# A decoder layer's expert stage: the experts' rows gathered by halves of the blocks, behind chosen stores

## The reference

```python
probs = softmax(xn @ Wr + br)                  # 8 experts
scores, idx = top_k(probs, 2)                  # two experts for each row
full = expert outputs relu(xn @ W1_e + b1_e) @ W2_e + b2_e
c = einsum('ef,efh->eh', relu(b1), W2) + b2;  c_total = c.sum(0)
out = sum(scores * (full[idx] - c[idx] + c_total))
return layernorm(x + residual + out)
```

## Time and profile before

| | us |
|---|---|
| median of 3 runs | 765.85 (764.94 to 766.87) |
| profiled execution | 768.75 |
| its span, first to last instruction | 767.0 |
| TensorE busy | 700.7 (91%) |
| VectorE busy | 472.1 (62%) |
| ScalarE busy | 332.5 (43%) |
| GpSimd busy | 265.8 (35%) |

### The profile page before, as it was taken

One profiled execution on the slowest core, in us unless ns is written; L12 is line 12 of the kernel. 1 busy time (PEld: TensorE's weight loads), 2 busy tenths in 40 slices (PEclk: granted clock), 3 DMA queues, 4 the chain that ended last, 5 costly groups with the idle time before them and its releaser, 6 DMA issues.

```text
span 767.0 us, 15113 instructions
## 1 busy us (share of the span) xinstructions
PE 700.7 (91%) x5090; PEld 610.8 (80%) x5091; DVE 472.1 (62%) x1094; ACT 332.5 (43%) x994; POOL 265.8 (35%) x216
## 2 busy tenths in 40 slices
PE   7799999999999999998998979999999999997980
PEld 7788897888989798896887858888888888786760
DVE  2635446577868778687858745555555555553476
ACT  5575767576676767676430212221222222121112
POOL 1200000120505033050546375176069300438664
PEclk9899999999999999999799899999999999998965
DMA  9367495641011020103141245255134411213125
GB/s 311 100 222 257 146 302 175 202 147 43 30 37 47 16 63 9 43 28 124 57 165 32 73 137 166 68 156 167 34 123 129 145 41 35 68 36 97 56 69 157
DMA packets 68496, 82.66 MB, mean 108 GB/s; under 512 B 5932, under 2 KB 59736, under 8 KB 68440
## 3 DMA queue, kind: packets, MB, share of 16 engines
q1 hardware_dynamic: 59800, 52.54, 21.4%
q0 software_dynamic: 8640, 29.38, 12.1%
HBM read 45.04 MB, written 36.86 MB: 107 GB/s over the span
## 4 chain that ended last, share of the span: by engine, by line
PE 73%; DVE 7%; ACT 7%; POOL 5%; issue 4%; DMA 2%; another core or an unknown queue 1%; POOLq 0%; SPq 0%; DVEq 0%; ACTq 0%
PE bank L1012 14%; PE bank L760 8%; PE bank L761 7%; PE bank L762 7%; PE bank L982 5%; PE bank L984 5%; PE bank L983 5%; PE bank L880 4%; PE bank L992 4%; PE bank L919 3%; PE bank L931 3%; ACT arena L1112 3%; POOL arena L729 2%; PE bank L968 1%
## 5 line engine op out<-in xcount | busy, mean ns | idle before, releaser
L1012 PE MATMUL bank<-w_ring,hidT_hi 128*128 x320 | 121.6, 413 | 6.2 <-DVE hidT_lo L1665 6.2
L1233 ACT ACTIVATE hidT_hi<-bank 128x512 fp32r<-128x512 f32 x80 | 43.5, 596 | 180.6 <-PE bank L992 171.0
L1112 ACT ACTIVATE arena<-bank,negmx 128x128 f32<-128x128 f32 x256 | 90.8, 377 | 6.2 <-DVE negmx L1268 6.2
L1012 PE MATMUL bank<-w_ring,hidT_lo 128*128 x320 | 84.2, 283 | 0.0
L1638 DVE TENSOR_TENSOR arena<-bank,b_rep 128x512 f32<-128x512 f32 x80 | 55.4, 692 | 42.9 <-PE bank L984 41.3
L1644 DVE TENSOR_REDUCE work<-bank 128x256 f32<-128x512 f32 x40 | 27.7, 692 | 85.1 <-PE bank L1012 77.5
L1012 PEld LDWEIGHTS bank<-w_ring,hidT_hi 128*128 128x128 f32 x320 | 61.1, 191 | 18.2 <-issue 6.9
L982 PE MATMUL bank<-w_ring,xgT_hi 128*128 x160 | 67.3, 421 | 4.6 <-DVE xgT_lo L1657 2.8
L632 POOL TENSOR_TENSOR rsq<-ssq,neghalf 128x8 f32<-128x8 f32 x8 | 13.2, 1646 | 145.4 <-DVE ssq L1368 145.4
L984 PE MATMUL bank<-w_ring,xgT_lo 128*128 x160 | 63.5, 397 | 0.0
L983 PE MATMUL bank<-w_ring,xgT_hi 128*128 x160 | 63.2, 395 | 0.0
(11 more groups left out here) (253 smaller groups left out, 1897.3 us busy)
## 6 DMA issues: line engine op xcount, KB each, us to landing
xg_dram<-zeros SPq DMA_DIRECT2D x9, 2176.0 KB, 8.8
w_raw<-in_L_ffn_W_dram POOLq DMA_DIRECT2D x16, 1024.0 KB, 6.1
y_dram<-zeros SPq DMA_DIRECT2D x2, 2560.0 KB, 10.7
work<-xg_dram SPq DMA_DIRECT2D x40, 128.0 KB, 2.1
y_dram<-work SPq DMA_DIRECT2D x40, 128.0 KB, 1.7
b_rep<-in_L_ffn_b_dram POOLq DMA_DIRECT2D x8, 512.0 KB, 4.2
work<-gmax_dram SPq DMA_DIRECT2D x14, 256.0 KB, 3.4
arena<-in_x_dram SPq DMA_DIRECT2D x8, 256.0 KB, 2.7
```

Of the source, the lines that this page charges most:

```text
L1012: last = pe.matmul(o, l, r, start=c == 0 and l is both[0], stop=c == FC - 1 and l is both[0])
L1112: last = nc.scalar.activation(probs[:, n % 2, h * S:(h + 1) * S], ps_score[:, h * S:(h + 1) * S], ACT.Exp, bias=negmx[:, n % 2, h:h + 1], ...
```

## The change

- GpSimd reads its counts before it waits for the weights of the last expert. There are now sixteen: for each half of the blocks (0 to 7, 8 to 15), each k and each of the four store semaphores.
- The low gathers of each half wait for the tile with that half's last row of expert 6, the high gathers for that of expert 7. Nothing waits for all 40 stores but a last wait at the end.
- GpSimd weighs three blocks of four (12 instead of 10). VectorE takes blocks 3, 7, 11 and 15 (`BY_DVE` = 3).
- The gather of the z rows moves behind the low rows. The four powers move behind all gathers.
- On VectorE the high row is added first (`add_high`, four blocks ahead) and TensorE's product after it; the first four stand between `dterm` and the constants. A quad is normalised after the next quad's `ve`.
- The router's counts of blocks 0 to 7 come from one more product on TensorE. `rows_of_y` makes sixteen counts.

```diff
-            for z in range(DEPTH):
-                pool.wait_ge(y_stored[z], pool.value_load(stored_by[0:1, z:z + 1], min_val=16,
-                                                          max_val=16 * (N_TILES // DEPTH + 1)))
-                pool.sem_inc(pool_seen, 1)
-            pool.indirect_dma_start(yz, None, y_dram, bass.IndirectOffsetOnAxis(ap=zslot[:, 0:1], axis=0))\
-                .then_inc(z_gathered, 16)
+            def rows_stored(h, k):
+                for z in range(DEPTH):
+                    pool.wait_ge(y_stored[z], stores[(2 * h + k) * DEPTH + z])
+                    pool.sem_inc(pool_seen, 1)
...
             for b in range(B):
-                gather(0, b, first_gathered if b < BY_DVE else low_gathered[b % 4])
-                if b >= BY_DVE + 2:
+                if b % 8 == 0:
+                    rows_stored(b // 8, 0)
+                gather(0, b, low_gathered[b % 4])
+                if b >= 2 and (b - 2) % 4 != BY_DVE:
                     add_low(b - 2)
-            for b in range(B - 2, B):
-                add_low(b)
+            add_low(B - 2)
+            for b in range(B):
+                if b % 8 == 0:
+                    rows_stored(b // 8, 1)
+                if b == 0:
+                    pool.indirect_dma_start(yz, None, y_dram, bass.IndirectOffsetOnAxis(ap=zslot[:, 0:1], axis=0))\
+                        .then_inc(z_gathered, 16)
+                gather(1, b, gathered[b // 2])
+            for q in range(QUADS):
+                rstd_of(q)
             for z in range(DEPTH):
                 pool.wait_ge(y_stored[z], 16 * (N_TILES // DEPTH + 1))
-            for b in range(B):
-                if b % 4 == 1 and b >= 8:
-                    rstd_of(b // 4 - 2)
-                gather(1, b, gathered[b // 2])
-            for q in range(2, QUADS):
-                rstd_of(q)
...
                     if p == PAIRS - 1:
-                        last = pe.matmul(dst[:, 2 * E:3 * E], ones[:, :], chosen_sum[:, B, :], start=True, stop=True)
+                        pe.matmul(dst[:, 2 * E:3 * E], ones[:, :], chosen_sum[:, B, :], start=True, stop=True)
+                        last = pe.matmul(dst[:, 3 * E:3 * E + 4], ones[:, :], chosen_sum[:, B // 2:B + 1:B // 2, E - 2:E],
+                                         start=True, stop=True)
...
+            def add_high(b):
+
+                z = y_all[:, 0, b, :]
+                dve.wait_ge(gathered[b // 2], 16 * 2)
+                if b % 4 != BY_DVE:
+                    dve.wait_ge(low_added, b - b // 4 + 1)
+                dve.scalar_tensor_tensor(z, y_all[:, 1, b, :], share[:, 1, b:b + 1], z, ALU.mult, ALU.add)\
+                    .then_inc(high_added, 1)
...
             for q in range(QUADS):
                 for b in range(4 * q, 4 * q + 4):
-                    z = y_all[:, 0, b, :]
-                    dve.wait_ge(gathered[b // 2], 16 * 2)
+                    dve.wait_ge(high_added, b + 1)
+                    constants_in(b)
+                    if b + 4 < B:
+                        add_high(b + 4)
                     dve.wait_ge(part_read, b + 1)
-                    chain.link(dve.scalar_tensor_tensor(z, y_all[:, 1, b, :], share[:, 1, b:b + 1], z, ALU.mult, ALU.add))
-                    last = dve.bn_stats(stats4[:, b % 4, :], z)
-                    if b + 4 < B:
-                        if b + 4 >= BY_DVE:
-                            dve.wait_ge(low_added, b + 5 - BY_DVE)
-                        constants_in(b + 4)
-                    if q and b % 4 == 1:
-                        normalise_out(q - 1)
+                    last = dve.bn_stats(stats4[:, b % 4, :], y_all[:, 0, b, :])
```

More of the change, by code:

```diff
@@ L173, in decoder_layer @@
         tile_f, first_f = (carve(work, N_TILES) for _ in range(2))
-        n1, tiles_e, ends, apart = (carve(work, E) for _ in range(4))
+        tiles_e, ends, apart = (carve(work, E) for _ in range(3))
+        n1, upto = carve(work, E + 4), carve(work, 4)
         assert off[0] <= 1024
@@ L232, in decoder_layer @@
         share, part_of = (sb(name, [P, 2, B]) for name in ("share", "part_of"))
-        stored_by = sb("stored_by", [P, DEPTH], I32)
+        stored_by = sb("stored_by", [P, 4 * DEPTH], I32)
         y_first = sb("y_first", [P, E])
@@ L346, in decoder_layer @@
         low_gathered = [sem(f"low_gathered{k}") for k in range(4)]
-        first_gathered = sem("first_gathered")
         low_weighed = sem("low_weighed")
+        high_added = sem("high_added")
         low_added = sem("low_added")
@@ L372, in decoder_layer @@
         LOOPED = N_TILES - 12
-        BY_DVE = 6
+        BY_DVE = 3
         assert LOOPED % DEPTH == 0
@@ L707, in _ @@
             pool.wait_ge(route_ready, 1)
+            stores = []
             for e in range(RING, E):
+                if e == E - 1:
+                    stores = [pool.value_load(stored_by[0:1, at:at + 1], min_val=16, max_val=16 * (N_TILES // DEPTH + 1))
+                              for at in range(4 * DEPTH)]
                 pool.wait_ge(y_done, pool.value_load(tile_end[0:1, e - RING:e - RING + 1], min_val=1, max_val=N_TILES))
@@ L734, in add_low @@
                 low = y_all[:, 0, b, :]
-                pool.wait_ge(low_gathered[b % 4], 16 * ((b - BY_DVE) // 4 + 1))
+                pool.wait_ge(low_gathered[b % 4], 16 * (b // 4 + 1))
                 pool.tensor_tensor(low, low, share[:, 0, b:b + 1].broadcast_to([P, D]), ALU.mult).then_inc(low_weighed, 1)
-                pool.wait_ge(low_weighed, b - BY_DVE + 1)
+                pool.wait_ge(low_weighed, b - b // 4 + 1)
                 pool.tensor_tensor(low, low, xres[:, b, :], ALU.add).then_inc(low_added, 1)
@@ L1467, in find_slots @@
                 if p == PAIRS - 1:
-                    chain.link(dve.tensor_scalar(n1, ring(un)[0][:, 2 * E:3 * E], 1.0, None, ALU.add))
+                    chain.link(dve.tensor_scalar(n1, ring(un)[0][:, 2 * E:3 * E + 4], 1.0, None, ALU.add))
                 dve.tensor_tensor(rank, ring(un)[0][:, 0:2 * E].rearrange("p (b e) -> p b e", e=E),
@@ L1580, in _ @@
             w_cnt = wide[:, 0:E * MAX_E_TILES].rearrange("p (e j) -> p e j", e=E)
-            chain.link(dve.tensor_tensor(w_cnt, n1.unsqueeze(2).broadcast_to([P, E, MAX_E_TILES]),
+            chain.link(dve.tensor_tensor(w_cnt, n1[:, 0:E].unsqueeze(2).broadcast_to([P, E, MAX_E_TILES]),
                                          iorow[:, 0:MAX_E_TILES].unsqueeze(1).broadcast_to([P, E, MAX_E_TILES]),
@@ L1624, in rows_of_y @@
                 chain.link(dve.tensor_tensor(share[:, 1, :], part_of[:, 0, :], part_of[:, 1, :], ALU.add))
[L1626 to L1630, removed]
+                chain.link(dve.tensor_scalar(upto, n1[:, E:E + 4], -1.0, 1.0 / P, ALU.add, ALU.mult))
+                upto2 = upto.rearrange("p (h k) -> p h k", k=2)
+                chain.link(dve.tensor_tensor(upto2, upto2, ends[:, E - 3:E - 1].unsqueeze(1).broadcast_to([P, 2, 2]), ALU.add))
+                shape = [P, 4, N_TILES]
+                by = wide[:, 0:4 * N_TILES].rearrange("p (k j) -> p k j", j=N_TILES)
+                chain.link(dve.tensor_tensor(by, iotile[:, :].unsqueeze(1).broadcast_to(shape),
+                                             upto.unsqueeze(2).broadcast_to(shape), ALU.is_le))
+                count = tile_f[:, 0:4 * DEPTH]
+                chain.link(dve.tensor_reduce(count.rearrange("p (k z) -> p k z", z=DEPTH),
+                                             wide[:, 0:4 * N_TILES].rearrange("p (k j z) -> p k z j", j=N_TILES // DEPTH, z=DEPTH),
+                                             AX.X, ALU.add))
+                dve.tensor_scalar(stored_by[:, :], count, 16.0, 16.0, ALU.mult, ALU.add).then_inc(y_rows_ready, 1)
             dve.wait_ge(out_cleared, 32)
@@ L1689, in _ @@
                 tile(j, j % DEPTH, min(2, N_TILES - 1 - j))
[L1692 to L1697, removed]
             def constants_in(b):
@@ L1712, in normalise_out @@
                 last.then_inc(out_ready, 1)
+            def add_high(b):
[5 more added lines that the diff above has]
+                    .then_inc(high_added, 1)
+            dve.wait_ge(z_gathered, 16)
+            dve.wait_ge(b2_loaded, 16)
+            dve.tensor_tensor(dterm, yz, b2_sb, ALU.add).then_inc(c_ready, 1)
             dve.wait_ge(input_doubled, 1)
-            dve.wait_ge(first_gathered, 16 * BY_DVE)
-            for b in range(BY_DVE):
+            for b in range(BY_DVE, B, 4):
+                dve.wait_ge(low_gathered[BY_DVE], 16 * (b // 4 + 1))
                 last = dve.scalar_tensor_tensor(y_all[:, 0, b, :], y_all[:, 0, b, :], share[:, 0, b:b + 1], xres[:, b, :],
@@ L1720, in _ @@
             for b in range(4):
-                constants_in(b)
+                add_high(b)
+            dve.wait_ge(csum_done, 1)
+            chain.link(dve.tensor_tensor(b2_sb, b2_sb, dterm, ALU.subtract))
+            dve.tensor_tensor(yz, b2_sb, bank[2][0:E, 0:D], ALU.add).then_inc(dterm_ready, 1)
             for q in range(QUADS):
```

(17 more changed lines are left out.)

## The result

| | before | after |
|---|---|---|
| median (lowest to highest) | 766.36 us (764.94 to 769.84), 4 runs | 757.95 us (757.13 to 761.07), 4 runs |
| ratio | | 0.9886 (0.9852 to 0.992) |
| profiled execution | 768.75 | 758.46 |
| its span | 767.0 | 756.5 |

What follows compares the result with a forecast made beforehand. GpSimd's gathers after the last tile were taken as the bound, VectorE next. A 4.5 us tail gain less 0.2 for small edits, pause kept, gave 764.4 us profiled; 2.9 lower against the median, 761.5 us; range 753 to 765.

Steps and rivals of the forecast that it cites:

- the likeliest case: Whole kernel: tail shorter by 4.5 us, pause near tile 35 kept at 7.2 us; 761.5 us, chance 0.46.
- rival 1: Tiles near 35: the 7.2 us pause goes as gathers no longer run back to back; 754.4 us, chance 0.32.
- signs of being wrong: `add_high` waiting on `gathered`, tiles slowing beside 17 more gathers, or first `constants_in` waiting much longer for TensorE.
- The gates: GpSimd's store waits: first low gather at 680.6 instead of 690.18, low phase 36.0 us, high gathers done at 739.7.
- The pause, taken as kept: VectorE and ScalarE stall near tile 35: assumed 7.2 us before and after; bounds gone (-7.2) or twice (+7.2).
- Rival 2: Tiles 35 and 39: instruction packets meeting gathers pause the tiles twice, 7.2 us more; 768.7 us, chance 0.12.
- To `dterm_ready`: VectorE's start of the tail: `dterm`, four weighted additions, four `add_high`, link, constants; ready at 734.7 against 733.49.
- First `constants_in`: VectorE's wait for TensorE's first part in the tail: starts 1.2 us after `dterm_ready`, at 735.9.
- The quads: VectorE's four groups of blocks in the tail: 5.0, 5.45, 5.45 and 3.8 us, at 1.10 a block.
- the four `rstd` behind them are off the path: GpSimd's powers after the high gathers: 8 us of slack at `add_high(15)`, so they delay nothing.
- The end: Last `ve` at 755.4 to span's end at 762.5, with ScalarE's blocks and two stores; 0.6 for sharing engines.
- The small edits: Router product on TensorE adds 0.2 us; `rows_of_y`'s extra 0.8 us on VectorE hides ahead of `xgT_lo`.

Runs made afterwards that it cites:

- b_mixed_2: Kernel before with only GpSimd's split of low additions from after (three blocks of four, from the third low gather), third chip: 759.84 us, ratio 0.9896.
- a_run_2: Kernel after with its first ten low gathers issued in a row, third chip: 774.52 us, ratio 1.0089.
- a_gate40: Kernel after with the high gathers waiting for all 40 stores again, second chip: 762.07 us, ratio 0.9952.
- a_best: Kernel after with quad 0's power between high gathers 12 and 13, and VectorE also weighing blocks 13 and 14: 759.74 us, ratio 0.9925.
- a_rstd: Kernel after with quad 0's power between high gathers 12 and 13 instead of behind all gathers: 758.63 us, ratio 0.9895.

## Why the prediction was right, and where it was not

The sign was right, and 757.95 lies in the range of 753 to 765. That the number came out is in part luck: the likeliest case (761.5, given 0.46) did not come, rival 1 (754.4, given 0.32) did, and the range held both. The gain of 8.4 us was forecast as 4.3, with two errors that work against each other: 7.2 us of pause that were taken as kept, and 2.8 us of tail that did not come. One of the prediction's own signs of being wrong appeared: `add_high` waits on `gathered`, for 1.78 us.

- **The gates.** Right. First low gather 680.23, low phase 36.2 us, to 716.4 (36.0 foretold, to 716.6), last high gather 738.40. It moved 16.9 us up: the 756.3 that the prediction gives for it before is the start of a power, and the gather stands at 755.32. Nothing in the sum rests on that. The counts cost nothing at their new place. GpSimd is off the end but for two waits, below.
- **The pause, taken as kept.** Wrong, and worth 7.2 us. The step that failed is "taken nearer to kept, because the pause stands beside such a packet": the packet was there without a pause in after. The other coincidence, ten gathers in a row, is the one that `b_mixed_2` and `a_run_2` bear out. It was given the smaller chance since nine gathers in a row left VectorE at its pace in the tail. That tells little of the tiles: in the tail of `a_gate40` VectorE kept its pace beside sixteen of them up to 742.04.
- **Rival 2, twice.** It didn't come in after, where the low gathers are split and the high ones stand beside the last reduction for 3.8 us only (716.84 to 720.63). `a_best`, whose run began 8.1 us ahead of the last reduction, did pause there, and `a_run_2` has both pauses that the rival spoke of: it names a real danger, with the wrong trigger.
- **To `dterm_ready`: 4.6 us foretold, 6.3 measured** (721.24 to 727.57). The missing 1.78 is the wait for the rows of blocks 2 and 3. It was free in the sum, since the high gathers start by tile 34's store and GpSimd's low phase, which don't move, while `dterm` moved 8.8 us up with the pause and the drift. Rival 1's sum asked only after `add_high(15)`, not after the first ones.
- **First `constants_in`**: 1.38 us after `dterm_ready`, 1.2 foretold. Right.
- **The quads: 5.0, 5.45, 5.45, 3.8 foretold; 4.76, 4.84, 7.06, 4.14 measured**, from the first `constants_in` and then from `ve` to `ve`. The pitch of a block was right (1.06 for 1.10). Quad 2's 1.6 too much is the 1.74 wait for quad 0's power: "the four `rstd` behind them are off the path" was wrong. The last gather is issued at 738.40, so the power of quad 0, possible since 733.9, starts at 739.37; VectorE asks for it behind quad 1's `ve` (738.55). Again the sum had it late enough only with the pause.
- **The end**: 6.75 us from the last `ve`, 7.1 foretold.
- **The small edits** can't be seen in any row by themselves; `xgT_lo` of tile 0 waited 0.90 for 1.44 before, so 0.5 of the added work on VectorE is hidden there, as foretold.

So the tail was forecast at -4.5 and gave -1.7: 1.8 for a gather, 1.7 for a power, less 0.7 in small terms. These are the waits in the trace, not what their removal would give: `a_rstd` took the second away and gained nothing that its runs show. With the pause gone, 761.5 - 7.2 + 2.8 = 757.1, within 0.9 of the measured median.

## What to carry to other kernels

When a profile has a stall that no dependency explains, price it as a case of its own and look for what in the change touches its neighbourhood; here an incidental edit, GpSimd's additions beginning six gathers earlier, carried 6.5 of 8.2 us where both were measured on one chip. When a case shifts one engine against another (a pause that goes moves VectorE up, not GpSimd), every wait between the two has to be worked out again for that case, first ones as well as last. And measure on more than one chip: the kernel before differed by 7 us (0.9%) between the chips, which is most of what this change brings, and after has no run on the chip where before was fast.

## What the runs showed of the hardware

- A run of ten indirect gathers issued every 1.25 us while tiles are in work delayed VectorE by 5.7 us and ScalarE by 5.4 in both traces of before, with their input from TensorE ready. No kernel traced on the first chip of the experiments was delayed, three of them with such a run. Where a gather was mostly followed by 1.3 us of GpSimd's own arithmetic (after, `b_mixed_2`), the tiles weren't delayed.
- A gather's issue of 0.95 us grows where it stands beside VectorE's unbroken row of operations on `arena`, `share` and `xres`; it then ended 0.82 to 0.84 us behind the end of that row. It took 2.17 at 721.88 in after (row from 721.57 to 723.23), 2.48 in before (733.42 to 735.86), 3.04 at 724.36 in `a_best` (724.13 to 726.57), and 2.54 at 733.41 in `a_run_2` (733.46 to 735.11). One gather in `b_mixed_2` took 0.98 beside such a row (725.83; row from 725.46), so this doesn't always happen. VectorE's own pitch stays 0.41. The Trainium skill (SBUF — State Buffer, Who interferes with whom) has it that a VectorE instruction with two SBUF inputs contends with a GpSimd instruction that reads SBUF. By the same section of the Trainium skill it is the order of issue that decides who blocks. The traces agree that the two meet. In all four it is GpSimd that gives way, by 1.2 to 2.1 us, in `a_run_2` too, where the gather began 0.05 us ahead of the row; so the order is not borne out there.
